# A fused attention and expert layer: GpSimd's inverse square roots by its power operation, the opening loads split and reordered, and a new order of work

## What is computed

```python
x = x + attn(_layernorm(x), ...)          # in attn: q = layernorm(q, q_gamma, q_beta), k likewise:
    (x - mu) * jax.lax.rsqrt(var + 1e-5) * gamma + beta
    attn = softmax(where(mask, scale * q @ k.T, -inf));  out = (attn @ v) @ Wo.T + bo
x = x + ffn(_layernorm(x), ...)           # _layernorm: (x - m) / sqrt(v + 1e-5)
    y = sum over the 2 chosen experts of weight * ((silu(x@We1+be1) * (x@We3+be3)) @ We2 + be2)
```

## Time and profile before

| | |
|---|---|
| median of 3 runs | 390.1 us (388.71, 390.1, and one outlier of 1749.16) |
| the profiled execution | 388.73 us, of it the span that the profile shows: 386.7 us |
| busy | PE 88%, DVE 73%, ACT 62%, POOL 47% of the span |

### The profile page before, as it was taken

How to read it: one execution, slowest core, us unless ns; L and a number is a source line. 1 busy time by engine, 2 the same in 40 slices (tenths; PEclk the granted TensorE clock), 3 DMA queues, 4 the chain that set the end, 5 groups by cost and what they waited for, 6 DMA issues and landing times.

```text
span 386.7 us, 8032 instructions
## 1 busy us (share of the span) xinstructions
PE 340.4 (88%) x2931; PEld 150.9 (39%) x2931; DVE 282.6 (73%) x496; ACT 240.7 (62%) x352; POOL 180.2 (47%) x304
## 2 busy tenths in 40 slices
...
GB/s 78 201 179 89 164 1 14 100 56 3 90 81 3 3 6 150 185 22 0 31 1 2 135 37 54 2 3 2 30 0 30 2 3 159 63 3 0 4 23 27
DMA packets 25687, 19.64 MB, mean 51 GB/s; under 512 B 9585, under 2 KB 22418, under 8 KB 25586
## 3 DMA queue, kind: packets, MB, share of 16 engines
...
q10 hardware_dynamic: 1392, 1.05, 1.2%
...
## 4 chain that ended last, share of the span: by engine, by line
PE 65%; DVE 12%; DMA 6%; POOL 5%; SPq 4%; issue 3%; ACT 3%; DVEq 0%; ACTq 0%; POOLq 0%
PE psum L705 14%; PE psum L753 12%; PE psum L682 9%; PE psum L769 8%; PE psum L659 8%; PE psum L633 6%; DVE mx_diag L1162 4%; DMA xs<-in_x 3%; PE psum L615 3%; DMA q_st<-parts 1%; SPq L505 1%; DVE mx_full L1162 1%; PE psum L773 1%; ACT probs L835 1%; PE psum L624 1%
## 5 line engine op out<-in xcount | busy, mean ns | idle before, releaser
L835 ACT ACTIVATE probs<-psum 128x1024 f32<-128x1024 f32 x144 | 142.6, 1023 | 42.5 <-PE psum L682 21.5
L1162 DVE TENSOR_REDUCE mx_diag<-psum 128x4 f32<-128x512 f32 (+2 forms) x96 | 96.6, 1043 | 25.9 <-PE psum L659 24.7
L1162 DVE TENSOR_REDUCE mx_full<-psum 128x2 f32<-128x1024 f32 x64 | 76.8, 1222 | 17.7 <-PE psum L659 17.3
L705 PE MATMUL psum<-probs,v_ones 128*18 128x512 f32 (+3 forms) x768 | 75.3, 490 | 0.0
L753 PE MATMUL psum<-x2T,w 128*128 128x512 f32 x144 | 71.4, 612 | 1.1 <-ACT mv L898 1.1
L633 PE MATMUL psum<-masks 64*128 64x128 bf16 (+2 forms) x896 | 51.2, 215 | 12.7 <-DMA q_st<-parts 5.6
L659 PE MATMUL psum<-k_st,q_st 62*128 62x512 bf16 (+3 forms) x384 | 59.5, 341 | 1.2 <-DVE mv L1241 0.8
L682 PE MATMUL psum<-q_st,k_st 64*128 64x512 bf16 (+3 forms) x384 | 53.4, 327 | 2.3 <-DVE mx_diag L1162 0.9
L633 PEld LDWEIGHTS psum<-masks 64*128 64x128 bf16 x896 | 33.6, 96 | 44.8 <-DVE mx_diag L1162 14.3
L1080 POOL TENSOR_SCALAR mh<-mh 128x512 f32<-128x512 f32 x27 | 16.7, 620 | 45.5 <-ACT mh L888 45.5
L1087 POOL TENSOR_TENSOR mh<-mh,mv 128x512 f32<-128x512 f32 x27 | 34.2, 1269 | 7.5 <-DVE mv L1241 7.0
...
## 6 DMA issues: line engine op xcount, KB each, us to landing
...
k_st<-in_c_pad SPq DMA_DIRECT2D x2, 512.0 KB, 11.1
...
xs<-in_x SPq DMA_DIRECT2D x3, 256.0 KB, 13.0
...
```

Source lines behind the costliest of these rows:

```text
L705: last = pe.matmul(acc[32 * j:32 * j + 2 * VC, q0:q0 + cols], own_then_zeros, probs[:, n % P_RING, j % 2, col:col + cols], start=(kt == 0 ...
L835: act.activation(probs[:, n % P_RING, :, :], wpair("scores", (s, i)), ACT.Exp, scale=SCALE).then_inc(exp_done, 1)
L1162: dve.tensor_reduce(dst[:, a % 2, :, pairs[0]:pairs[0] + nm, qt], w, AX.X, ALU.max, negate=True).then_inc(max_free, 1)
```

## The change

Three edits, and a new ORDER around them.

1. POOL's inverse roots take one tensor_tensor instruction with ALU.pow (exponent -0.5, from a tile `minus_half` that POOL fills at the start) and one Newton step: 7 instructions for 128 columns instead of 15, 9 for 4 columns instead of 17.
2. The loads: Wo, the gate's weights and bo leave the head of SP's queue; chunk 1's input goes ahead of the masks; the pads are cut from 4 transfers (2 of 512 KB, 2 of 256 KB) into 12 of 128 KB, of which 4 (those that chunk 0's maxima read) go ahead of the inputs of chunks 2 and 3, and 8 behind them, then Wo, the gate's weights and bo. These 11 have a semaphore `ld_rest`.
3. New waits for all of `ld_rest`: PE before `weights2` (the transposes of Wo and the gate's weights), PE before group a = 4 (the first of sequence 1), POOL before `xbo.0`.

```diff
-N_ATTN, N_ROPE, N_PAD, N_MOE = 7, 6, 4, 15
+N_ATTN, N_ROPE, N_PAD, N_REST, N_MOE = 5, 5, 4, 11, 15
@@ sync
-for w, dst in ((Wq, 0), (Wk, 1), (Wv, 2), (Wo, 3)):
+for w, dst in ((Wq, 0), (Wk, 1), (Wv, 2)):
...
-sp.dma_start(gate_raw[:, :], gate_w).then_inc(ld_attn, 16)
...
-sp.dma_start(bo_b[:, :], bo.partition_broadcast(P)).then_inc(ld_rope, 16)
+sp.dma_start(xs[:, 1, :, :], x_v[B]).then_inc(ld_x[1], 16)
 sp.dma_start(masks...)
-for i in range(1, NX):
+for t in range(N_TERMS, HD):
+    pad(k_st[t::HD, 0, :, 0:CH], ld_pad)
+    pad(q_st[t::HD, 0, :, :], ld_pad)
+for i in range(2, NX):
     sp.dma_start(xs[:, i, :, :], ...)
-    if i == 1:
-        for t in range(N_TERMS, HD):
-            sp.dma_start(k_st[t::HD, :, :, :]..., c_pad).then_inc(ld_pad, 16)
-            sp.dma_start(q_st[t::HD, :, :, :]..., c_pad[:, 0:H // 2 * CH]).then_inc(ld_pad, 16)
+for t in range(N_TERMS, HD):
+    pad(k_st[t::HD, 0, :, CH:S], ld_rest)
+    for c in range(2):
+        pad(k_st[t::HD, 1, :, c * CH:(c + 1) * CH], ld_rest)
+    pad(q_st[t::HD, 1, :, :], ld_rest)
+sp.dma_start(w_raw[:, 3, :], Wo).then_inc(ld_rest, 16)
+sp.dma_start(gate_raw[:, :], gate_w).then_inc(ld_rest, 16)
+sp.dma_start(bo_b[:, :], bo.partition_broadcast(P)).then_inc(ld_rest, 16)
@@ tensor: weights2, maxima
+pe.wait_ge(ld_rest, 16 * N_REST)
...
+if a == NG and u == 0:
+    pe.wait_ge(ld_rest, 16 * N_REST)
@@ gpsimd: head_rstd (norm_rstd alike)
-link(pool.tensor_scalar(seed_pool[:, :], v.bitcast(I32), -0.5, RSQRT_SEED, ALU.mult, ALU.add))
+link(pool.tensor_tensor(y, v, minus_half[:, :], ALU.pow))
 link(pool.tensor_scalar(v, v, -0.5, 0.0, ALU.mult, ALU.add))
-for step in range(3):
-    ...
+link(pool.tensor_tensor(t, y, y, ALU.mult))
+link(pool.tensor_tensor(h, t, v, ALU.mult))
+link(pool.tensor_scalar(t, h, 1.0, 1.5, ALU.mult, ALU.add))
+link(pool.tensor_tensor(hrstd[:, :], y, t, ALU.mult))
```

The ORDER is new from end to end; the set of stages is the same. Its opening, before and after, up to the first `exp` (stages that the prediction speaks of):

```diff
-norm.0 ones.0 weights.0@2 xT.0@0 ... qkv.0@5 tables.0 qkv.1@6 qkv.2@1 qkv.3@4 norm.1 norm_rstd.1
-qkv_read.0 ... qkv_read.3 weights2.0@2 weights2_read.0 norm_apply.1 xT.1@6 headsum.0 headrstd.0
-xT_read.1 qkv.4@6 ... norm.2 ... norm_rstd.2 ... qkv_read.7 rope.0
-qT.0@4 norm_apply.2 qT_lead.0 qT_rest.0 kT.0@2 kT_lead.0 qT_mid.0 qT_low.0 xT.2@0 ... kT_rest.0
-stack.0.0.1 stack.0.0.0 norm.3 kT_mid.0 stack_act.0.1.0 stack.0.0.2 headsum.1 stack_act.0.1.1 kT_low.0 stack_act.0.1.2
-max.0.0@23 ... max.1.2@45 rstd_pool.1 rope_pool.1 ... mneg.0 ... rope_join.1 ... mrow.0 scores.0.0@23 exp.0.0
+ones.0 weights.0@3 weights_read.0 norm.0 tables.0 norm.1 xT.0@6 norm.2 xT_read.0 qkv.0@3 ... qkv.3@5
+qkv_read.0 ... qkv_read.3 headsum.0 norm_rstd.1 norm_rstd.2 norm_apply.1 xT.1@5 xT_read.1 weights2.0@2
+weights2_read.0 qkv.4@4 ... qkv_read.7 headrstd.0 rope.0
+norm_apply.2 tables_pool.0 headsum.1 qT.0@2 qT_lead.0 norm.3 kT.0@5 kT_lead.0 stack.0.0.0 xT.2@6 xT_read.2 qkv.8@4
+qT_rest.0 qT_mid.0 stack.0.0.1 kT_rest.0 rstd_pool.1 kT_mid.0 stack_act.0.1.1 stack_act.0.1.0 qT_low.0 qkv.9@1 kT_low.0
+rope_pool.1 rope_join.1 stack_act.0.1.2 stack.0.0.2 max.0.0@23 ... max.1.2@23 ... qT.1@4 ... mneg.0 kT.1@6 ...
+... qT_rest.1 ... kT_rest.1 ... headsum.2 ... rstd_pool.2 ... max.2.2@23 max.2.3@01 maxred.2.2 mrow.0 scores.0.0@45 ... exp.0.0
```

More of the change, by code:

```diff
@@ L138 @@
[L138 to L167, removed]
@@ L253 @@
-moe_y.3.5 wide.3.7@5 wide.3.8@1 moe_h_dve.3.7 moe_h_dve.3.8 moe_y.3.6 moe_y.3.7 moe_y.3.8 y_leave.3 yturn.3@3 final.3
+ones.0 weights.0@3 weights_read.0 norm.0 tables.0 norm.1 xT.0@6 norm.2 xT_read.0 qkv.0@3 qkv.1@4 qkv.2@0 qkv.3@5
+qkv_read.0 qkv_read.1 qkv_read.2 qkv_read.3 headsum.0 norm_rstd.1 norm_rstd.2 norm_apply.1 xT.1@5 xT_read.1 weights2.0@2
+weights2_read.0 qkv.4@4 qkv.5@2 ones.1 qkv_read.4 qkv.6@6 qkv_read.5 qkv_read.6 qkv.7@1 qkv_read.7 headrstd.0 rope.0
+norm_apply.2 tables_pool.0 headsum.1 qT.0@2 qT_lead.0 norm.3 kT.0@5 kT_lead.0 stack.0.0.0 xT.2@6 xT_read.2 qkv.8@4
@@ new lines @@
+qT_rest.0 qT_mid.0 stack.0.0.1 kT_rest.0 rstd_pool.1 kT_mid.0 stack_act.0.1.1 stack_act.0.1.0 qT_low.0 qkv.9@1 kT_low.0
+rope_pool.1 rope_join.1 stack_act.0.1.2 stack.0.0.2 max.0.0@23 maxred.0.0 qkv_read.8 qkv_read.9 max.0.1@45 maxred.0.1
+max.0.2@01 qkv.10@6 qkv_read.10 max.0.3@23 maxred.0.2 maxred.0.3 max.0.4@45 maxred.0.4 max.0.5@01 max.1.0@45 maxred.0.5
+maxred.1.0 max.1.1@01 max.1.2@23 maxred.1.1 maxred.1.2 qT.1@4 qT_lead.1 stack.1.0.0 mneg.0 kT.1@6 kT_lead.1 mturn.0@1
+mcopy.0 qT_rest.1 qT_mid.1 norm_rstd.3 qT_low.1 kT_rest.1 kT_mid.1 kT_low.1 norm_apply.3 max.1.3@23 max.1.4@01
@@ new lines @@
+maxred.1.3 max.1.5@45 maxred.1.4 maxred.1.5 qkv.11@6 xT.3@1 max.2.0@23 qkv_read.11 headsum.2 maxred.2.0 xT_read.3
+max.2.1@45 maxred.2.1 mneg.1 mturn.1@0 stack.1.1.0 qkv.12@6 mcopy.1 rstd_pool.2 rope_pool.2 max.2.2@23 max.2.3@01
+maxred.2.2 mrow.0 scores.0.0@45 maxred.2.3 max.2.4@23 maxred.2.4 qkv_read.12 exp.0.0 scores.0.1@45 exp.0.1 max.2.5@01
+maxred.2.5 qkv.13@6 mneg.2 stack.1.0.1 mrow.1 stack.1.1.2 stack.1.1.1 qkv_read.13 scores.1.0@45 exp.1.0 max.3.0@01
+maxred.3.0 max.3.1@23 pv.0 scores.1.1@01 max.3.2@45 maxred.3.1 exp.1.1 maxred.3.2 scores.2.0@23 exp.2.0 qkv.14@6
```

226 lines of the change are left out of this document (123 added, 103 removed).

## The result

The changed kernel took 441.8 us (441.3 to 442.4), the kernel before 389.4 beside it: ratio 1.135, 95% interval 1.133 to 1.137. It is 52 us slower, where I had forecast 382.5 and a range of 376 to 390.

A forecast was written before the change was run, and what follows sets the result against it. PE was taken as the bound from about 64 us on, with a long chain of waits before it. The profiled 388.7 less 5.6 (head) less 1.0 (idle PE) gave 382.1; forecast 382.5 us, range 376 to 390.

The forecast's parts named there:

- The power: POOL's 128-column roots: one power takes 1.27 us, bounded by 0.46 and 2.36, so `head_rstd` 4.0 us, 2.9 less.
- rival (c): POOL's 128-column roots: slower if the power costs over 4.1 us; at 8 us each, 395 us in all; chance 0.08.
- Its size at 4 columns: POOL's `norm_rstd`: a power of 4 columns at 0.3 us (0.22 to 2.36), the root 2.6 us in place of 5.1.
- my sum: Whole kernel: 388.7 less 5.6 (head) less 1.0 (idle PE won back behind the head by earlier roots) is 382.1 us.
- The root beside DVE's two-input products: POOL's chunk-2 root: 9.1 us beside DVE's rotary products in place of 5.1; the new order puts it before `rope.0`.
- The loads: Head: tables from about 9.4, chunk 2's input at 16.5 in place of 24.8, SP's last load at 32.5 to 34.
- The wait for `ld_rest`: PE before `weights2`: ends at 23.5, giving back 2.7 us of a gain of 5.7, and 5 at worst.
- From the head to the end: Behind the first maximum: its 5.6 us lead stays, through PE work done meanwhile in time that was idle.
- rival (d): PE behind the head: new order has other gaps of the same size, head's gain given back, 388 to 392; chance 0.12.
- the sign: PE from 63.6 us on: idle time of 13 to 15 us would show the forecast right.
- The first scores: End of the head: they come at 61.5, only about 2 us sooner than 63.58, after some 3.8 us more DVE work.

The follow-up runs named there:

- e1: The changed kernel with its loads and its ORDER, but POOL's inverse roots of before (integer guess, three Newton steps): 399.1 us, ratio 1.028.
- e10: New loads and roots of before, with the new ORDER up to and with `exp.0.0`, then the ORDER of before: 388.7 us, ratio 0.999.
- e4: The kernel before with the new loads and their waits, its ORDER and roots kept: 385.9 us, ratio 0.992.
- e11: New loads and roots of before, with the new ORDER up to and with `norm2.2`, then the ORDER of before: 395.4 us, ratio 1.016.
- e2: The changed kernel with the power only in the six roots of 4 columns, the three of 128 columns as before: 392.5 us.

## Why the prediction was wrong, by its own steps

The steps, each as the difference of two medians (the median of the kernel before was between 388.8 and 389.4 in the four sets of measurements, and the executions of e1 spread over 5 us and those of e10 over 3, so a step is good to a microsecond or so; the three steps of the ORDER hold only in this order of taking them):

| step | us |
|---|---|
| the kernel before | 389.1 |
| the new loads (e4) | -3.2 |
| the new ORDER to `exp.0.0` (e10) | +2.8 |
| ... to `norm2.2` (e11) | +6.7 |
| ... to the end (e1) | +3.7 |
| the power at 4 columns, six times (e2) | -6.5 |
| the power at 128 columns, three times (the changed kernel) | +49.3 |
| sum | 441.9 |

**The power.** This is the term that failed: "above that the longest POOL instruction of any kind, 2.36 us". The mechanism of rival (c) was right, with its break-even at 4.1 us, the place (`qT_low.0` behind `rstd_pool.1`, two more roots ahead of `mneg`) and the sign; its price was not, since it reckoned with 8 us where 20.8 came, and its chance of 0.08 came from the same bad bound. With 20.8 in the rival's own working, `qT_low.0` follows the root at 55.0 (measured 55.07), the first maximum comes some 13 us late, and the two further roots hold the scores for 16.7 us each: 388.7 + 13 + 33, an estimate of 435 us, against 441.8. (The rival itself took 6 us for two roots of 3.9 each, which are 7.8.) Nothing in a trace bounds an operation that isn't in it. The durations of adds and products only bound other adds and products: a product of 128 columns takes 0.46 us or so, under 4 ns a column, and the power's slope is 160 ns.

**Its size at 4 columns** was wrong by a factor (1.02 for 0.3), and there the effect was better than forecast: `norm_rstd` fell to 3.3 us, where I had 2.6, and its gain of 6.5 us in the new ORDER was not in my sum, which took 1 us for the roots behind the head. (Undisturbed, the old root takes 4.7 us in e1, which is what 17 times 0.28 makes, and not the 5.1 that I had.)

**The root beside DVE's two-input products** was read rightly. In the changed kernel chunk 2's root runs before `rope.0` at 0.19 to 0.26 us an instruction (its power apart), and `tables_pool.0`, now beside `rope.0`, takes up to 1.31 us where it took 0.32 alone:

```profile
21.58 0.33 POOL L449 TENSOR_TENSOR g_cos<-rope,gb 128x64 f32<-128x64 f32 x1
21.85 1.31 POOL L450 TENSOR_TENSOR g_sin<-rope,gb_rot 128x64 f32<-128x64 f32 x1
...
28.35 0.32 POOL L452 TENSOR_TENSOR mh<-rope,gb_rot 128x64 f32<-128x64 f32 x1
```

The Trainium skill, "GPSIMD Engine Reference", 8 Key points, says that GpSimd shares its SBUF interfaces with VectorE and that the two collide where VectorE's instruction has two SBUF inputs; these rows agree (1.31 against 0.32 us).

**The loads** were right: every landing within 1.2 us of its forecast, SP's last load 2 us sooner than I took, and the first maximum of e1 at 42.7 against 42.5. The wait for `ld_rest` did what was said (3.65 us of PE's waiting before L619, ended at 23.17). Its price was booked too low, as 2.7 us: by my own 24.3 for `qkv.4` against 20.8 without it, it is 3.5, and `qkv.4` started at 23.79. What it alone costs was not tried, and it may hold e4 back: there PE waits 6.5 us for it.

**From the head to the end** was the second step that failed: "So the 5.6 stay." They stay only if the work behind keeps its own pace, and I took a list that is new from end to end as if it did. The runs show that the new one loses 10.4 us behind `exp.0.0` once its own head stands before it (and 21.6 behind the old head); in e1's trace 10.4 us of PE's waits are for `x2T.1` to `x2T.3` and `qT.2`, where e4 has 1.1. That was my rival (d), "with other gaps of the same size"; the gaps were larger (23.3 us after 63.6 in e1, outside the 13 to 15 that I had named as the sign), and I had left out that a gap can cost a second time, in the clock behind it. The first scores, for which I had 61.5, came about 62 in e1 (the first exponential at 62.98 in place of 64.41 before), so 5.4 us of lead at the first maximum were 1.4 there; I had said that they stay all the same, through the PE work done meanwhile. e10 shows that they don't: with the body of before its first maximum is 5.8 us sooner than in the kernel before, and its time is the same (388.7 against 388.8).

What stays open is what each gap is worth. The runs locate the loss in three stretches and e1's trace names the stages before which PE stands, but no single stage was moved by itself.
